# Fused attention and FFN on one core: the first Wo product and the second half of the values leave the bank they share with the score maxima

## Chip, cores and metric

One NeuronCore of a Trainium2 chip. The time is device microseconds of one launch, the median of several runs; lower is better. TensorE (PE) multiplies, PEld is its weight load, VectorE is DVE, ScalarE is ACT, GpSimd is POOL, SyncE is SP.

## The reference

A block of a transformer in float32 over x of 4 x 1024 x 128: attention with 16 heads of 64, added to x, then a gated FFN of width 352 whose inputs and weights are quantised to FP4 and back in blocks of 16, added again.

```python
q, k, v = heads(ln(x) @ Wq.T), heads(ln(x) @ Wk.T), heads(ln(x) @ Wv.T)
attn = exp(s - max(s)); attn /= sum(attn) + 1e-10      # s = q k^T / 8
x = x + (attn @ v) @ Wo.T + bo
h = silu(fp4(ln(x)) @ fp4(w_gate).T) * (fp4(ln(x)) @ fp4(w_up).T)
x = x + fp4(h) @ fp4(w_down).T
```

Every row's maximum is subtracted before the exponential, so it has to be computed from the scores before the scores are computed again, transposed, for the exponential.

## The kernel before

The unit of work is a pair of heads of one batch: 4 batches x 8 pairs = 32 pairs, one round each (r = 1 to 32), with a round 0 ahead that only prepares and a round 33 behind that only finishes. All values are split in a high and a low half-precision part, so that a product is made of several matmuls.

A round has four units k = 0 to 3 (two heads, two halves of 512 query rows) and every unit eight slots s = 0 to 7 (128 keys each). A place in a round is written (k, s). In every slot:

- TensorE computes the transposed scores (L628, L630) into one of two banks `st`, ScalarE takes their exponential (L781), GpSimd its low part (L475). TensorE also multiplies the unit before by the values (L650, L655, L657) into the bank `ob`.
- In slots 0 and 4, TensorE first computes plain scores of the unit ahead for the maxima (`scores`, L610): two pairs of matmuls, each over two banks of the four of `sm`: the first pair in banks 2 and 3, the second in banks 0 and 1. VectorE reduces each pair to a row maximum (L959, written to `negm`) in slots 0, 1, 4 and 5.

Everything else is a **job** of the list `JOBS`: its name, its bank, and its places on TensorE, on ScalarE and on VectorE. There are three banks for jobs: `MB` is their own; `X0` and `X1` are banks 2 and 3 of `sm`, shared with the plain scores. A job is issued at the end of its slot on TensorE (`job`). ScalarE takes it ahead of its exponential of that slot, VectorE behind its reduction of that slot (the two functions `take`). All engines work through these places in program order.

What a job waits for on TensorE is worked out from the list. `job_before` finds the job that had its bank last, and `maxima_ahead` the last maximum taken from the shared banks. In `MB` a job waits until the job before it has been taken (`taken`). In `X0` and `X1` it waits for whichever came later, the job before or the first maximum of the last pair (L533 to L537). In turn `scores` waits until the last jobs in X0 and X1 have been taken (L599 to L602).

The jobs that the change and the prediction speak of:

- `m`: transposes of the maxima (L577), at slot 0 of each unit, in MB; ScalarE and VectorE take it (L732, L920), and SyncE places it by DMA.
- `t0`, `t1`: transposes of the finished outputs' halves (L559), in X1, taken by ScalarE (`oT`, L716). `t1` is at (1, 5).
- `o0`, `o1`: the Wo product of each half (L564), four products, added to x by VectorE (L940). `o0` needs `t0`'s copy.
- `v0`, `v1`: the halves of the next pair's values (L553), 12 matmuls each, the high part taken by ScalarE (L719), then the low part by VectorE (L925).
- `x` (in even rounds from 10) and `h0` (in odd rounds from 11): transposes for the FFN (L1253, L1264), taken by ScalarE (L1276; L1281 and L1282). The FFN of two tiles of rows is spread over two or three rounds, an even one and the odd ones about it; its quantisation runs on VectorE (`quant`, L1088 on) at fixed places, such as (0, 2), (0, 3), (0, 6), (1, 2), (1, 3) and the next round's for the hidden values (`AT_H`), and (3, 6) for their first steps (`AT_H_BEGIN`).
- `w0`, `w1`, `w2`: transposes of the quantised FFN weights in rounds 5, 7 and 8 (L1172, L1170).

Of the kernel before, what the change touches and what calls it, by code (L numbers as in the profile page):

```python
# [49 lines left out]
MB, X0, X1 = range(3)  # L50
JOBS = [("m", MB, (0, 0), (0, 1), (0, 0)), ("k0", X0, (0, 1), (0, 2), (0, 2)), ("k1", MB, (0, 2), (0, 3), (0, 3)),
        ("q0", MB, (0, 4), (0, 5), (0, 5)), ("q1", X0, (0, 5), (0, 6), (0, 6)),
        ("m", MB, (1, 0), (1, 1), (1, 0)), ("t0", X1, (1, 1), (1, 2), None), ("x", MB, (1, 3), (1, 4), None),
        ("o0", X0, (1, 5), None, (1, 6)), ("t1", X1, (1, 5), (1, 6), None), ("h0", MB, (1, 6), (1, 7), None),
        ("m", MB, (2, 0), (2, 1), (2, 0)), ("g0", X0, (2, 1), (2, 2), (2, 2)), ("h1", X1, (2, 1), (2, 2), None),
        ("w0", X1, (2, 1), (2, 2), None), ("w2", X1, (2, 1), (2, 2), None), ("u0", X1, (2, 2), None, (2, 3)),
        ("o1", MB, (2, 3), None, (2, 4)), ("d", X0, (2, 5), None, (2, 6)), ("n0", X0, (2, 5), (2, 6), (2, 6)),
        ("m", MB, (3, 0), (3, 1), (3, 0)), ("g1", X0, (3, 1), (3, 2), (3, 2)), ("w1", X1, (3, 1), (3, 2), None),
        ("n1", X1, (3, 1), (3, 2), (3, 2)), ("u1", X1, (3, 2), None, (3, 3)), ("v0", MB, (3, 3), (3, 4), (3, 4)),
        ("v1", X0, (3, 5), (3, 6), (3, 6))]  # L60
ON_PE, ON_ACT, ON_DVE = 2, 3, 4


# [1438 lines left out]
```

How the kernel before makes its waits and increments, by code:

```python
def wait(eng, sem, n):  # L87
    if isinstance(n, int) and n <= 0:
        return
    eng.wait_ge(sem, n)
# [259 lines left out]
            def round_(g, r, q):  # L351
# [3 lines left out]
                    head, half = (k + 1) // 2 % 2, (k + 1) % 2
                    n, u = 2 * (q if k < 3 else 1 - q) + head, (k + 1) % 2
                    wait(sp, s_mr, 4 * (g - 1) + k + 2)
                    for part, rows in enumerate((m_high, m_low)):
                        sp.dma_start(q_hm[n][part:part + 1, half * HALF:(half + 1) * HALF]
                                     .rearrange("a (t i) -> a t i", t=IT), rows[u][:, :]).then_inc(s_md[u], 16)
                if r == 0:
                    sp.wait_ge(s_qz, 4)
                if cur:
                    place_max(0)
                if nxt:
# [35 lines left out]
        @block.gpsimd  # L404
        def _(pool):
            pool.memset(half[:, :], -0.5).then_inc(s_hf, 1)
            pool.memset(minus[:, :], -1.0).then_inc(s_hf, 1)
            pool.memset(eps[:, :], LN_EPS).then_inc(s_hf, 1)
            pool.memset(ident[:, :], 0.0).then_inc(s_id, 1)
            pool.wait_ge(s_id, 1)
            pool.affine_select(out=ident[:, :], in_=ident[:, :], compare_op=ALU.not_equal, fill=1.0,
                               base=0, pattern=[[-1, P]], channel_multiplier=1).then_inc(s_id, 1)
            for n in range(4):
# [2 lines left out]
                pool.memset(q_hm[n][0:DH, :].bitcast(F32), 0.0).then_inc(s_qz, 1)  # L416
            ffn.constants(pool)
            pool.wait_ge(s_hf, 3)
```

## Time and profile before

| | |
|---|---|
| median of 3 runs | 1441.13 us (1439.35 to 1445.4) |
| the profiled execution | 1440.82 us |
| its span, first to last instruction | 1437.8 us |
| mean granted TensorE clock | 0.982 of full speed |
| busy: PE, DVE, ACT, POOL | 1341.8 (93%), 1123.0 (78%), 1134.4 (79%), 1143.5 us (80%) |
| chain that ended last, by engine | PE 69%, DVE 21%, ACT 6%, issue 3% |

PE is the busiest engine, but a busy share is an average. Which engine holds up the others is seen from the waits and the timeline: for every instruction they give the idle time of its engine ahead of it, and whose work ended it.

### The profile page before, as it was taken

To read this page: it belongs to the slowest core of one execution; us is meant where nothing else is said; L and a number is where in the kernel's file an instruction comes from. 1 tells how busy PE (TensorE), PEld (TensorE's weight loads), DVE (VectorE), ACT (ScalarE), POOL (GpSimd) and SP (SyncE) were. 2 spreads that over 40 slices of the span, in tenths; PEclk is the share of its full clock that TensorE was granted. 3 is DMA by queue.
4 is the path that set the end of the run, shared out by engine and by line. 5 is a ranking of instruction groups with operands and counts; after the bars stand their busy time and mean duration, and the time that the engine had idled before them with its cause. 6 is when DMAs were issued, how large, how long until landed. Compare 5 with 4: busy or idle time off the path is not lost.

```text
span 1437.8 us, 43018 instructions
## 1 busy us (share of the span) xinstructions
PE 1341.8 (93%) x17924; PEld 880.5 (61%) x17924; DVE 1123.0 (78%) x1717; ACT 1134.4 (79%) x2285; POOL 1143.5 (80%) x1135
## 2 busy tenths in 40 slices
PE   3899999999999999999999999999999999999956
PEld 2466666666666666666666666666666666666644
DVE  7777777778778878787887878888787888878677
ACT  2698887978888887888788888888888888788842
POOL 5688988878888878788887888888888888888832
PEclk8899999999999999999999999999999999999986
DMA  7111111112211111122111111211122121112000
GB/s 178 46 46 46 46 41 28 28 42 46 46 46 46 29 44 28 46 50 46 46 28 34 40 46 45 50 35 38 24 49 46 46 50 24 42 31 50 2 5 15
DMA packets 46687, 60.26 MB, mean 42 GB/s; under 512 B 8672, under 2 KB 21920, under 8 KB 46496
## 3 DMA queue, kind: packets, MB, share of 16 engines
q1 hardware_dynamic: 46336, 57.26, 17.0%
q8 instruction: 143, 2.34, 0.7%
q14 instruction: 48, 0.39, 0.1%
q10 hardware_dynamic: 160, 0.26, 0.1%
HBM read 4.80 MB, written 2.10 MB: 5 GB/s over the span
## 4 chain that ended last, share of the span: by engine, by line
PE 69%; DVE 21%; ACT 6%; issue 3%; DMA 1%; POOL 1%; SPq 0%; DVEq 0%
PE st L628 13%; PE st L630 11%; DVE negm L959 8%; PE sm L610 8%; PE ob L650 7%; PE ob L657 6%; PE ob L655 6%; ACT probs L781 3%; PE sm L548 2%; PE sm L1258 2%; PE mb L564 2%; PE sm L564 2%; DVE qv L1113 2%; PE mb L548 2%; PE sm L553 2%
## 5 line engine op out<-in xcount | busy, mean ns | idle before, releaser
L475 POOL TENSOR_TENSOR p_low<-probs 128x512 f16<-128x512 f32 x1024 | 1080.3, 1075 | 231.7 <-ACT probs L781 214.2
L781 ACT ACTIVATE probs<-st,lift,exp_scale 128x512 f32<-128x512 f32 x1024 | 775.3, 772 | 164.2 <-PE st L630 156.3
L959 DVE TENSOR_REDUCE negm<-sm 128x1 f32<-128x1024 f32 x512 | 616.2, 1214 | 204.8 <-PE sm L610 204.5
L628 PE MATMUL st<-q_hl,k_hh 128*128 128x512 f16 x1024 | 391.9, 383 | 6.8 <-ACT probs L781 6.7
L630 PE MATMUL st<-q_hm,k_l 128*128 128x512 f16 x1024 | 388.9, 380 | 0.0
L655 PEld LDWEIGHTS ob<-v,probs 128*128 128x128 bf16 x4096 | 289.7, 99 | 60.9 <-ACT o_raw L750 1.1
L655 PE MATMUL ob<-v,probs 128*128 128x65 f16 x4096 | 319.3, 193 | 0.7 <-ACT o_raw L750 0.7
L657 PE MATMUL ob<-v,probs 128*128 128x64 f16 x4096 | 319.8, 194 | 0.0
L657 PEld LDWEIGHTS ob<-v,probs 128*128 128x128 bf16 x4096 | 270.6, 97 | 59.9
L650 PEld LDWEIGHTS ob<-v,p_low 128*128 128x128 f16 x4096 | 177.1, 97 | 90.7 <-issue 1.1
L628 PEld LDWEIGHTS st<-q_hl,k_hh 128*128 128x128 f16 x1024 | 99.5, 97 | 154.3 <-issue 80.4
L650 PE MATMUL ob<-v,p_low 128*128 128x65 f16 x4096 | 188.1, 193 | 0.0
L610 PE MATMUL sm<-k_hh,q_hl 64*128 64x512 f16 x512 | 155.7, 384 | 10.7 <-DMA q_hm<-q_high 3.8
L610 PE MATMUL sm<-k_hh,q_hm 64*128 64x512 f16 x512 | 156.2, 385 | 0.0
L791 ACT ACTIVATE o_n<-o_raw,rden 128x64 f32<-128x64 f32 x512 | 147.1, 337 | 1.1 <-DVE rden L948 1.1
L630 PEld LDWEIGHTS st<-q_hm,k_l 128*128 128x128 f16 x1024 | 100.2, 98 | 26.8 <-issue 9.5
L716 ACT ACTIVATE oT<-sm 128x512 f32<-128x512 f32 x64 | 38.2, 597 | 37.4 <-PE sm L559 37.0
L946 DVE TENSOR_SCALAR den<-o_raw 128x4 f32<-128x4 f32 x128 | 51.4, 402 | 8.4 <-ACT o_raw L750 8.4
L564 PE MATMUL sm<-wo_s,oT 128*128 128x128 f32 x256 | 36.8, 287 | 20.7 <-DVE negm L959 19.3
L610 PEld LDWEIGHTS sm<-k_hh,q_hl 64*128 64x128 f16 x512 | 29.1, 94 | 34.5 <-issue 11.2
L750 ACT ACTIVATE o_raw<-ob 128x260 f32<-128x260 f32 x128 | 50.0, 390 | 0.0
L564 PEld LDWEIGHTS sm<-wo_s,oT 128*128 128x128 f32 x256 | 31.2, 192 | 22.5 <-DVE negm L959 20.9
(204 smaller groups left out, 1640.6 us busy)
## 6 DMA issues: line engine op xcount, KB each, us to landing
k_hh<-k_high SPq DMA_DIRECT2D x128, 128.0 KB, 2.4
k_l<-k_low SPq DMA_DIRECT2D x64, 128.0 KB, 2.4
q_hl<-q_high SPq DMA_DIRECT2D x64, 128.0 KB, 2.3
q_hl<-q_low SPq DMA_DIRECT2D x64, 128.0 KB, 2.4
q_hm<-q_high SPq DMA_DIRECT2D x62, 128.0 KB, 2.3
x<-x SPq DMA_DIRECT2D x4, 512.0 KB, 7.3
q_hm<-m_high SPq DMA_DIRECT2D x128, 1.0 KB
q_hm<-m_low SPq DMA_DIRECT2D x128, 1.0 KB
```

Source lines behind the costliest of these rows:

```text
L475: return pool.tensor_tensor(p_low[b][:, j, :], p, p.bitcast(BF16)[:, 1::2], ALU.subtract)
L548: last = pe.matmul(bank[:, :], of_pair(wT[w], "qk".index(name[0]), g), of_batch(xT[a], g, c * HALF, HALF), start=(w == 0 and a == 0), stop ...
L564: last = pe.matmul(bank[:, t * P:(t + 1) * P], oT[:, (4 * c + t) * P:(4 * c + t + 1) * P], wo_s[:, bass.ds((g - 2) % PAIRS, 1), :].rearran ...
L610: last = pe.matmul(sm_banks[2 * (1 - a) + h], q_rows[rows, t * P:(t + 1) * P], k_hh[n][rows, h * 512:(h + 1) * 512], start=True, stop=True)
L628: pe.matmul(st[s % 2][:, :], k_hh[n][:, s * P:(s + 1) * P], q_hl[n][:, half * HALF:(half + 1) * HALF], start=True, stop=False)
L630: pe.matmul(st[s % 2][:, :], k_l1[n][:, s * P:(s + 1) * P], q_hm[n][:, half * HALF:(half + 1) * HALF], start=False, stop=True).then_inc(s_ ...
L650: last = pe.matmul(ob[:, o:o + VC], p_low[1 - k % 2][:, j, t * P:(t + 1) * P], v_j[:, 1:1 + VC], start=False, stop=(j == JT - 1), skip_gro ...
L655: pe.matmul(ob[:, o:o + VC], p, v_j[:, 1:1 + VC], start=(t == 0 and j == 0), stop=False, skip_group_check=True)
L657: pe.matmul(ob[:, o + 1:o + VC], p, v_j[:, 1 + VC:1 + VC + DH], start=False, stop=False, skip_group_check=True)
L781: nc.scalar.activation(probs[k % 2][:, s, :], st[s % 2][:, :], ACT.Exp, bias=lift[:, 0:1], scale=exp_scale[:, head, pair:pair + 1]).then_i ...
L791: last = nc.scalar.activation(o_n[pq][:, tile + t, head * DH:(head + 1) * DH], o_raw[k % 2][:, t, 1:VC], ACT.Copy, scale=rden[:, k % 2, t: ...
L959: nc.vector.tensor_reduce(negm[k % 2][:, pair % 4:pair % 4 + 1], banks.rearrange("p a n -> p (a n)"), AX.X, ALU.max, negate=True).then_inc ...
```

## The change

Four jobs change bank or place, and no instruction is added or removed. The first Wo product `o0` goes from X0 in slot 5 to MB in slot 4 of unit 1, and its addition on VectorE from slot 6 to slot 5. The second half of the values `v1` goes from X0 in slot 5 to MB in slot 6 of unit 3, and is taken in slot 7 in place of 6. To make room in MB, the transposes `x` come one slot earlier, and `h0` goes from MB to X0 at its old place.

```diff
-        ("m", MB, (1, 0), (1, 1), (1, 0)), ("t0", X1, (1, 1), (1, 2), None), ("x", MB, (1, 3), (1, 4), None),
-        ("o0", X0, (1, 5), None, (1, 6)), ("t1", X1, (1, 5), (1, 6), None), ("h0", MB, (1, 6), (1, 7), None),
+        ("m", MB, (1, 0), (1, 1), (1, 0)), ("t0", X1, (1, 1), (1, 2), None), ("x", MB, (1, 2), (1, 3), None),
+        ("o0", MB, (1, 4), None, (1, 5)), ("t1", X1, (1, 5), (1, 6), None), ("h0", X0, (1, 6), (1, 7), None),
...
-        ("v1", X0, (3, 5), (3, 6), (3, 6))]
+        ("v1", MB, (3, 6), (3, 7), (3, 7))]
```

## Rows read from the trace of the kernel before

**Rows 1.** Waits of TensorE: us in total, times, longest us.

```profile
PE sm L564 <- DVE negm L959: 19.3, 13, 2.4
PE sm L553 <- DVE negm L959: 9.0, 13, 1.1
```

**Rows 2.** Timeline, round 23, (1, 5) to (2, 0): start, us, engine, line, operation.

```profile
968.61 0.38 PE L628 MATMUL st<-q_hl,k_hh 128*128 128x512 f16 x1
...
969.88 2.34 DVE L959 TENSOR_REDUCE negm<-sm 128x1 f32<-128x1024 f32 x2
...
971.15 1.16 PE L564 MATMUL sm<-wo_s,oT 128*128 128x128 f32 x8 [1.45 <-DVE negm L959]
...
972.58 0.38 PE L628 MATMUL st<-q_hl,k_hh 128*128 128x512 f16 x1
...
974.20 0.27 ACT L1282 ACTIVATE hiddenT<-mb 96x128 f32<-96x128 f32 x1
...
974.62 0.09 PEld L610 LDWEIGHTS sm<-k_hh,q_hl 64*128 64x128 f16 x1
...
975.06 1.23 DVE L959 TENSOR_REDUCE negm<-sm 128x1 f32<-128x1024 f32 x1 [2.03 <-PE sm L610]
```

**Rows 3.** Timeline, round 32, (2, 3): the second Wo product, with nothing beside it.

```profile
1356.52 1.13 PE L564 MATMUL mb<-wo_s,oT 128*128 128x128 f32 x8
...
1357.49 0.38 PE L628 MATMUL st<-q_hl,k_hh 128*128 128x512 f16 x1
```

**Rows 4.** Timeline, round 23, the products of (3, 5), (3, 6) and (3, 7).

```profile
991.04 0.38 PE L628 MATMUL st<-q_hl,k_hh 128*128 128x512 f16 x1
...
992.64 0.67 DVE L925 TENSOR_TENSOR v<-mb,v 128x512 f16<-128x512 f32 x1
...
992.78 0.23 PE L553 MATMUL sm<-wT_high,xT_high 128*128 128x128 f16 x1 [0.66 <-DVE negm L959]
...
993.46 0.38 PE L628 MATMUL st<-q_hl,k_hh 128*128 128x512 f16 x1
...
994.13 0.38 PE L628 MATMUL st<-q_hl,k_hh 128*128 128x512 f16 x1
```

**Rows 5.** Timeline, round 24, (3, 5) to the next round's (0, 0).

```profile
1033.27 0.38 PE L628 MATMUL st<-q_hl,k_hh 128*128 128x512 f16 x1
...
1033.61 0.68 DVE L925 TENSOR_TENSOR v<-mb,v 128x512 f16<-128x512 f32 x1
...
1034.21 1.22 DVE L959 TENSOR_REDUCE negm<-sm 128x1 f32<-128x1024 f32 x1
...
1034.85 0.38 PE L628 MATMUL st<-q_hl,k_hh 128*128 128x512 f16 x1
...
1035.68 0.69 DVE L925 TENSOR_TENSOR v<-sm,v 128x512 f16<-128x512 f32 x1 [0.26 <-ACT v L719]
...
1036.29 0.88 DVE L1103 TENSOR_REDUCE q_small<-hidden 128x44 f32<-128x704 f32 x1
...
1037.20 0.28 DVE L1105 TENSOR_SCALAR q_small<-q_small 128x44 f32<-128x44 f32 x1
...
1037.40 0.09 PEld L577 LDWEIGHTS mb<-ident,negm 128*4 128x4 f32 x1
```

**Rows 6.** Timeline, (2, 0) and (2, 1): round 5 (two rows) and round 8.

```profile
222.06 1.23 DVE L959 TENSOR_REDUCE negm<-sm 128x1 f32<-128x1024 f32 x1
...
223.64 0.50 PE L1172 MATMUL sm<-ident,wgu 128*128 128x128 f32 x3
...
345.92 0.55 PE L1170 MATMUL sm<-ident,wd 128*128 128x128 f32 x3 [0.62 <-DVE negm L959]
```

**Rows 7.** Timeline, round 0, (3, 4), to the scores of round 1.

```profile
40.34 0.68 DVE L925 TENSOR_TENSOR v<-mb,v 128x512 f16<-128x512 f32 x1
...
40.48 0.29 PE L553 MATMUL sm<-wT_high,xT_high 128*128 128x128 f16 x1 [1.11 <-DVE negm L959]
...
43.56 0.58 PE L610 MATMUL sm<-k_hh,q_hl 64*128 64x512 f16 x1 [1.61 <-DVE v L925]
```

## The prediction

> **What bounds the kernel now.** I read the waits of TensorE first, then the timeline of one odd and one even round, slot by slot. TensorE is the engine whose idle time counts: it works almost without a gap through all rounds of attention, in program order, so a wait in its queue moves everything behind it. The list of its waits names the two that the change touches [rows 1]: the first Wo product (o0, L564 into the shared bank) stood 19.3 us in 13 rounds, the second half of the values (v1, L553) 9.0 us in 13 rounds, both for a maximum (negm, L959) on VectorE. The other rounds don't wait there at all. Those 28.3 us are about the most that the change could bring; what matters is what each of these instructions would wait for next.
>
> The timeline says where the 13 lie. Eleven of the waits of o0 are in the odd rounds 11 to 31, 1.45 us each [rows 2], where the quantisation of the hidden values has delayed VectorE; the remaining 3.3 us are in rounds 5 and 8. Twelve of the waits of v1 are in the odd rounds 9 to 31, 0.66 us each [rows 4], and one of 1.11 us is in round 0 [rows 7]. I use round 23 for the odd rounds and round 24 for the even ones.
>
> **First Wo product, odd rounds 11 to 31.** The products of slot 5 of unit 1 began at 968.61. VectorE served the two reductions of slot 4 and 5 from 969.88 to 972.22, the first until about 971.09, and o0 started at 971.15 [rows 2]. In its own bank o0 waits for no maximum: it goes in at 968.61, ahead of slot 5, and costs 0.97 us there, which is what the second Wo product takes alone (1356.52 to 1357.49) [rows 3]. Then come the products of slot 5, 0.90 us (a slot 5 with v1 and without a wait takes 1033.27 to 1034.85, 1.58 [rows 5], less 0.68 for v1 [rows 4]). They end at 968.61 + 0.97 + 0.90 = 970.48. **t1 (L559) stays in slot 5 and in the shared bank, so it inherits the wait for the same maximum** and stands until 971.15. It takes 0.46 us (o0 and t1 together took 971.15 to 972.58, 1.43 us [rows 2], less 0.97 for o0), so slot 6 begins at 971.61 in place of 972.58. The gain is 0.97 us a round: the length of o0, not the length of the wait. 11 x 0.97 = 10.7 us.
>
> Is it given back? Behind the two reductions VectorE sat idle for 2.03 us before the next one [rows 2], so a TensorE that comes 0.97 us sooner doesn't run into it. h0 moves the other way, into a shared bank: the scores at the start of unit 2 must now wait until ScalarE has copied it. That copy ended at 974.47 and the scores' weights went in at 974.62 [rows 2]. Both follow t1, so the distance of 0.15 us stays, less some 0.06 us from signal to start (971.09 to 971.15). I take nothing for it; if the cover is gone, the overrun costs in 12 rounds.
>
> In the rounds with no wait the change only takes o0 and t1 apart, on a TensorE that works on either side of them: same matmuls, nothing. The transposes x come one slot sooner in even rounds: same instructions, on a bank that ScalarE and VectorE have left two slots before, nothing. The addition of o0 on VectorE goes from slot 6 to slot 5, behind the same two reductions: nothing. No DMA moves, and SyncE's and GpSimd's lists stay as they are.
>
> **Rounds 5 and 8.** In both, VectorE has a quantisation of weights queued behind these reductions without a break, and TensorE meets it again in unit 2. In round 8 the transposes of w_down then stand 0.62 us for the next maximum [rows 6]: what o0 gives is paid there, gain 0. In round 5 that next maximum comes from 222.06 to 223.29 [rows 6] after a queue without idle time; the transposes behind it went in at 223.64 [rows 6], so TensorE can save some 0.35 us and no more. Between 0 and 0.97 us in each; I take 0.4 for the two.
>
> **Second half of the values, odd rounds 9 to 31.** It went in behind slot 5 and now goes in behind slot 6, into the own bank. Slot 5 with v1 takes 1.58 us without the wait [rows 5], and 2.42 in odd rounds (991.04 to 993.46) [rows 4]: the wait costs 0.84. After the change v1 is ready to go at 991.04 + 0.90 + 0.67 (slot 6, 993.46 to 994.13) = 992.61, and no maximum is in its way. But **the own bank still holds v0**, the first half: VectorE takes its low part from 992.64 to 993.31 [rows 4]. v1 starts at 993.37, takes 0.68, and slot 7 begins at 994.05 in place of 994.13. Of 0.84 us 0.08 are left: 12 x 0.08 = 1.0 us. In even rounds v0 has been taken by 1034.29, before v1 is ready at 1034.85 [rows 5]: no wait, no gain.
>
> The Trainium skill, page "PSUM — Partial Sum Buffer", section "Summary: rules for kernel authors", says that reading PSUM while matmuls run wants the matmuls in a different bank, and semaphores by bank. That speaks against this half of the change, since v0 and v1 had two banks and now share one. By that rule v1 comes out as above, 1.0 us; without it, with only the maximum in the way, it would be the first rival.
>
> What is late next: the transposes of the maxima (m, L577) at slot 0 of the next round use v1's new bank. In even rounds VectorE now has two steps of 0.88 and 0.28 us ahead of v1's low part; its reduction ends at 1035.43, so the low part (0.68) ends at 1037.15 to 1037.27, and m's weights went in at 1037.40 [rows 5]. That is a cover of 0.1 to 0.2 us: nothing, but thin. In odd rounds v1 is through at 994.05; copy and low part took 1.52 us behind it (1034.85 to 1036.37) [rows 5], so the bank is free at 995.6, while m comes 1.88 us after the start of slot 7 (1034.85 + 0.67 to 1037.40) [rows 5], at 995.9.
>
> **Round 0.** v1 waited for a maximum until 40.48 and the scores of round 1 for v1's low part, 1.61 us, until 43.56 [rows 7]. So v1 itself took 43.56 - 1.61 - 40.48 = 1.47 us. Now v1 waits for v0's low part (until 41.02 [rows 7]), is through at 41.08 + 1.47 = 42.55, and the scores follow at once: 1.0 us, between 0 and 1.6.
>
> **Sum.** 10.7 + 0.4 + 1.0 + 1.0 = 13.1 us. The profiled execution took 1440.8 us (its span 1437.8, and 3.0 around it), 0.3 under the median of 1441.1. 1441.1 - 13.1 = **1428.0 us**. About 0.5% (7.2 us) is what a measurement of this kernel can tell from no change, so "faster" means under 1433.9.
>
> **Rivals.** First, both waits go altogether for v1: 0.84 us in 12 rounds, 9.1 us more than I count: 1418.9. Against it: v0's low part stands in VectorE's list behind the late maximum [rows 4]. Chance 0.07.
> Second, the handover at the round's end costs: m waits for v1's low part. With 0.2 us beyond the cover in 31 rounds, 6.2 us: 1434.2, no change by the bound above. For it: the thin cover in rows 5. Chance 0.11.
> Third, h0's copy holds the scores of unit 2 by 0.1 to 0.4 us in 12 rounds, 1.2 to 4.8 us: 1429.2 to 1432.8. For it: the 0.15 us of rows 2. Chance 0.07.
> Fourth, on the other side: v1's low part comes late by about the length of a reduction (1.22 us [rows 5]). ScalarE copies the high part only after an exponential, VectorE waits for that copy, and its next reduction waits behind. m, the reduction and all that follows on TensorE would stand about 1.0 us in 31 rounds: 1428 + 31 = 1459. It decides from (13.1 + 7.2) / 31 = 0.65 us a round on. Against it: before the change both came within 1.52 us of v1's end, and 1.88 us are there now [rows 5]. Chance 0.04.
>
> **How the numbers follow.** Forecast 0.71. The range takes in the forecast, the third rival, the second up to its price and part of the way to the first, since the prices of round 0 and of rounds 5 and 8 could add up to 2.1 us: 1421 to 1434.5. Faster by over 0.5%: the forecast, the first and the third, 0.85. Within 0.5%: the second, 0.11. Slower: the fourth, 0.04.
>
> **What would show it.** In rounds 11 to 31 o0 starts right behind slot 4 with no idle time, and t1 in slot 5 has an idle time of about 0.6 us for negm. v1, now into mb, has an idle time of about 0.6 us in odd rounds, put down to v0's low part (L925), and none for a maximum. m has no idle time. Odd rounds from 11 on get 1.0 us shorter and even rounds keep their length. Idle time at m, or at the scores of unit 2 for L1282, would make me wrong.

## The result, and the profile after

The changed kernel took **1457.78 us** (median of 4 runs, 1454.72 to 1459.94), the kernel before beside it 1440.24 us (4 runs, 1439.06 to 1445.4). The ratio is 1.0121 with a 95% interval of 1.0106 to 1.0136: slower by 17.5 us, where 13.1 us less was forecast. The profiled execution took 1454.72 us, the shortest of the four; its span is 1452.9 us (1437.8 before), the mean granted clock of TensorE 0.982 as before. The other three show a mean granted clock of 0.979 to 0.980.

The page of the changed kernel, busy time by engine and the chain that ended last:

```profile
PE 1347.8 (93%) x17924; PEld 881.0 (61%) x17924; DVE 1160.9 (80%) x1717; ACT 1141.2 (79%) x2285; POOL 1140.0 (78%) x1135
PE 59%; DVE 31%; ACT 5%; issue 3%; DMA 1%; POOL 1%; SPq 0%; DVEq 0%
```

No instruction was added, and yet VectorE is busy 1160.9 us in place of 1123.0. Its share of the chain that ended last went from 21% to 31%, TensorE's from 69% to 59%. The 37.9 us of additional busy time are the trail to follow: **the same steps last longer.** First the waits of TensorE, in the changed kernel (us in total, times, longest us):

```profile
PE mb L548 <- DVE k_low L914: 21.9, 12, 2.8
PE mb L553 <- DVE v L925: 8.7, 13, 1.7
PE sm L559 <- DVE negm L959: 6.6, 12, 1.4
PE sm L1172 <- DVE negm L959: 3.8, 2, 2.8
PE mb L577 <- DVE v L925: 2.9, 11, 0.3
```

and of the kernel before, the two lines beside [rows 1] that answer to them:

```profile
PE mb L548 <- DVE k_low L914: 4.7, 12, 2.8
PE sm L1172 <- DVE negm L959: 0.9, 1, 0.9
```

The two waits of [rows 1], 28.3 us, are gone. t1 (L559) and v1 (L553) wait 6.6 and 8.7 us in their place. The new one is large and stands at a job that the change did not touch: **q0**, the first projection of the queries at slot 4 of unit 0 (L548 into the jobs' own bank), waits 21.9 us for the low part of k1 (L914), 4.7 before. The transposes of the maxima (m, L577) wait 2.9 us.

Where the rounds gained and lost, from the slots' starts (first L628 of each) in the two traces (means over the odd rounds 11 to 29 and the even rounds 10 to 30; round 31 of the changed kernel is an exception, 45.61 us):

| stretch | before | after |
|---|---|---|
| odd rounds from 11: slots (1, 4) and (1, 5) | 4.66 | 3.72 us |
| odd rounds: slots (3, 5) and (3, 6) | 3.09 | 3.01 |
| odd rounds: slot (1, 7), ahead of the scores that follow h0 | 1.55 | 1.62 |
| end of an odd round: (3, 7) and the next (0, 0) | 2.26 | 2.33 |
| end of an even round: (3, 7) and the next (0, 0) | 2.20 | 2.53 |
| odd rounds: slot (0, 4), with q0 | 1.68 | 3.24 |
| a whole odd round | 43.29 | 44.24 |
| a whole even round from 10 | 41.34 | 41.61 |
| round 0, from the span's start | 44.53 | 43.27 |
| round 5 | 42.94 | 45.21 |
| round 8 | 40.67 | 41.30 |

**Rounds 5 and 31 hold something else as well, the granted clock.** From the first slots of round 1 to the end of round 31 TensorE's granted clock is 1.00, but for a few short stretches at 0.50, the lower of its two levels (1.2 in place of 2.4 GHz). The kernel before has one, in round 5, in slots 5 to 7 of unit 1 (first line; the number ahead of the last two is the granted clock). The changed kernel has two, in round 5 at (2, 3) and in round 31 at (0, 4) and (0, 5):

```profile
217.70:221.00 3.30, 3.30 (x19) 2.15 (x19) 3.16 (x9) 1.96 (x3) 1.22 (x2) 0.50 0.00 0
224.30:227.60 3.30, 3.30 (x27) 2.80 (x24) 0.27 (x1) 1.58 (x4) 2.61 (x4) 0.50 0.00 1
1313.20:1316.50 3.30, 3.30 (x23) 1.72 (x22) 3.27 (x4) 2.16 (x3) 0.31 (x2) 0.50 0.56 130
```

With it slot (2, 3) of round 5 took 4.14 us in place of 2.53, and round 31 1.4 us more than the other odd rounds. Shortly ahead of the first TensorE had stood 2.83 us for a maximum, just ahead of the second 1.73 us for k1's low part; but the same waits stand in other rounds and runs with no such stretch behind them. So rounds 5 and 8 can't be compared by their lengths alone. The run with the cut in unit 3 alone, below, has the same instructions as the changed kernel up to round 8. There round 5 has no such stretch and takes 43.60 us, and round 8 has one and takes 42.87.

**The part of o0 went as forecast.** Round 23 of the changed kernel, TensorE from slot 4 to slot 6 of unit 1 (start us, us, then the instruction; in brackets the idle time ahead of it and what ended it):

```profile
978.68 0.39 PE L628 MATMUL st<-q_hl,k_hh 128*128 128x512 f16 x1
979.38 1.13 PE L564 MATMUL mb<-wo_s,oT 128*128 128x128 f32 x8
980.35 0.38 PE L628 MATMUL st<-q_hl,k_hh 128*128 128x512 f16 x1
981.91 0.66 PE L559 MATMUL sm<-ident,o_n 128*128 128x128 f32 x4 [0.48 <-DVE negm L959]
982.40 0.38 PE L628 MATMUL st<-q_hl,k_hh 128*128 128x512 f16 x1
```

o0 has no idle time ahead of it, t1 waits the rest of what o0 used to wait. Against [rows 2], with 0.69 us for slot 4, the two slots are 0.94 us shorter (0.97 forecast).

**The part of v1** takes the wait that was forecast, but VectorE behind it looks different. Round 23 again, slot 5 of unit 3 to the next round:

```profile
1002.52 0.68 DVE L925 TENSOR_TENSOR v<-mb,v 128x512 f16<-128x512 f32 x1
1003.17 2.04 POOL L475 TENSOR_TENSOR p_low<-probs 128x512 f16<-128x512 f32 x2 [0.40 <-ACT probs L781]
1003.25 0.23 PE L553 MATMUL mb<-wT_high,xT_high 128*128 128x128 f16 x1 [0.58 <-DVE v L925]
1004.25 1.25 DVE L1128 SCALAR_TENSOR_TENSOR qv<-qw,qv 128x256 f32<-128x256 f32 x1
1005.41 0.68 DVE L925 TENSOR_TENSOR v<-mb,v 128x512 f16<-128x512 f32 x1
1006.15 0.27 PE L577 MATMUL mb<-ident,negm 128*4 128x128 f32 x1
```

v1 waits 0.58 us for v0's low part. But the step of the quantisation between the two low parts, L1128, lasts 1.25 us; behind v1's low part, as it stood before the change, it lasted 0.41. It now ends 0.29 us after the second of two instructions of GpSimd that began at 1003.17. Here it still fits: m goes in at 1006.15 without idle time.

**In even rounds it doesn't fit.** The end of round 24 and what follows in round 25:

```profile
1045.36 0.88 DVE L1103 TENSOR_REDUCE q_small<-hidden 128x44 f32<-128x704 f32 x1
1046.23 1.04 POOL L475 TENSOR_TENSOR p_low<-probs 128x512 f16<-128x512 f32 x1
1046.27 1.05 DVE L1105 TENSOR_SCALAR q_small<-q_small 128x44 f32<-128x44 f32 x1
1047.23 0.68 DVE L925 TENSOR_TENSOR v<-mb,v 128x512 f16<-128x512 f32 x1
...
1047.96 0.27 PE L577 MATMUL mb<-ident,negm 128*4 128x128 f32 x1 [0.26 <-DVE v L925]
...
1051.76 0.71 DVE L1109 TENSOR_SCALAR q_small<-q_small 128x44 f32<-128x44 f32 x1
1052.95 1.04 POOL L475 TENSOR_TENSOR p_low<-probs 128x512 f16<-128x512 f32 x1 [0.52 <-ACT probs L781]
1052.97 1.77 DVE L1113 TENSOR_TENSOR qv<-hidden,q_small 128x704 f32<-128x704 f32 x1
1054.66 0.74 DVE L914 SCALAR_TENSOR_TENSOR k_low<-mb,k_scale,k_high 128x512 f16<-128x512 f32 x1
1055.46 0.39 PE L548 MATMUL mb<-xT_high,wT_high 128*128 128x512 f16 x1 [1.73 <-DVE k_low L914]
```

The same place before, VectorE and GpSimd (L1105 itself, 1037.20 and 0.28, is in [rows 5]):

```profile
1036.40 1.04 POOL L475 TENSOR_TENSOR p_low<-probs 128x512 f16<-128x512 f32 x1
...
1040.92 0.17 DVE L1109 TENSOR_SCALAR q_small<-q_small 128x44 f32<-128x44 f32 x1
1041.59 1.17 DVE L1113 TENSOR_TENSOR qv<-hidden,q_small 128x704 f32<-128x704 f32 x1
```

Set the starts against GpSimd's. L1105 began 0.04 us after an instruction of GpSimd (1046.23) and ended at 1047.32, 0.05 us after its end. Before, it began at 1037.20, 0.80 us into the instruction of 1036.40, and ended at 1037.48, 0.04 us after its end. **Both times it ended with GpSimd's instruction; 0.28 us was what was left of that, not what the step costs.** The groups by shape say that it is so in every round (us in total, mean ns), in the kernel before:

```profile
L1105 DVE TENSOR_SCALAR q_small<-q_small 128x44 f32<-128x44 f32 x12 | 4.0, 330 | 0.4
L1109 DVE TENSOR_SCALAR q_small<-q_small 128x44 f32<-128x44 f32 x12 | 2.8, 236 | 0.0
L1113 DVE TENSOR_TENSOR qv<-hidden,q_small 128x704 f32<-128x704 f32 x12 | 13.7, 1139 | 0.4
L1128 DVE SCALAR_TENSOR_TENSOR qv<-qw,qv 128x256 f32<-128x256 f32 x12 | 4.9, 409 | 0.0
```

and in the changed one:

```profile
L1105 DVE TENSOR_SCALAR q_small<-q_small 128x44 f32<-128x44 f32 x12 | 12.4, 1034 | 0.4
L1109 DVE TENSOR_SCALAR q_small<-q_small 128x44 f32<-128x44 f32 x12 | 8.7, 726 | 0.0
L1113 DVE TENSOR_TENSOR qv<-hidden,q_small 128x704 f32<-128x704 f32 x12 | 20.4, 1703 | 0.4
L1128 DVE SCALAR_TENSOR_TENSOR qv<-qw,qv 128x256 f32<-128x256 f32 x12 | 14.9, 1244 | 0.0
```

Nor is there an exception in the traces of all thirteen kernels. Every L1105 and L1109 of 128 x 44 elements that took over 0.23 us, 169 in all, ended 0.04 us after the instruction of GpSimd that was running when it began. The larger steps end later by a fixed part of their own work: L1128 (128 x 256) by 0.28 us, L1131 and L1135 (128 x 384) by 0.41 or 0.42, L1113 (128 x 704) by 0.74 or 0.75.

The four groups above are 31.0 us of the additional busy time. L1105, L1109 and L1113 stand ahead of the low part of k1 on VectorE, and q0 needs that low part.

### The profile page after: what moved, and what is told of

Same layout as the page of the kernel before. It is cut to its first block, busy times and chain, and to the rows that moved or that the text cites. A ratio compares the mean times of both kernels' runs of the same rounds, so it can differ in the third digit from the quotient of the medians.

```text
span 1452.9 us, 42989 instructions
## 1 busy us (share of the span) xinstructions
PE 1347.8 (93%) x17924; PEld 881.0 (61%) x17924; DVE 1160.9 (80%) x1717; ACT 1141.2 (79%) x2285; POOL 1140.0 (78%) x1135
## 4 chain that ended last, share of the span: by engine, by line
PE 59%; DVE 31%; ACT 5%; issue 3%; DMA 1%; POOL 1%; SPq 0%; DVEq 0%
DVE negm L959 12%; PE st L628 11%; PE st L630 9%; PE sm L610 6%; PE ob L657 5%; PE ob L655 5%; PE ob L650 5%; ACT probs L781 3%; PE mb L564 3%; DVE qv L1113 2%; PE sm L1258 2%; PE sm L548 2%; DVE v L925 2%; PE mb L548 2%; DVE qv L1128 2%
## 5 line engine op out<-in xcount | busy, mean ns | idle before, releaser
L959 DVE TENSOR_REDUCE negm<-sm 128x1 f32<-128x1024 f32 x512 | 615.6, 1213 | 199.1 <-PE sm L610 199.0
L628 PE MATMUL st<-q_hl,k_hh 128*128 128x512 f16 x1024 | 392.0, 383 | 7.1 <-ACT probs L781 6.9
L628 PEld LDWEIGHTS st<-q_hl,k_hh 128*128 128x128 f16 x1024 | 99.6, 97 | 151.8 <-issue 81.1
L564 PE MATMUL mb<-wo_s,oT 128*128 128x128 f32 x512 | 73.4, 287 | 1.4 <-ACT oT L716 1.4
L946 DVE TENSOR_SCALAR den<-o_raw 128x4 f32<-128x4 f32 x128 | 63.2, 493 | 9.0 <-ACT o_raw L750 9.0
L564 PEld LDWEIGHTS mb<-wo_s,oT 128*128 128x128 f32 x512 | 63.1, 194 | 1.7 <-issue 1.7
L553 PE MATMUL mb<-wT_high,xT_high 128*128 128x128 f16 x256 | 46.9, 221 | 10.2 <-DVE v L925 8.7
L925 DVE TENSOR_TENSOR v<-mb,v 128x512 f16<-128x512 f32 x64 | 43.5, 680 | 8.5 <-ACT v L719 8.5
```

What stands on the lines that cost most here:

```text
L564: last = pe.matmul(bank[:, t * P:(t + 1) * P], oT[:, (4 * c + t) * P:(4 * c + t + 1) * P], wo_s[:, bass.ds((g - 2) % PAIRS, 1), :].rearran ...
L628: pe.matmul(st[s % 2][:, :], k_hh[n][:, s * P:(s + 1) * P], q_hl[n][:, half * HALF:(half + 1) * HALF], start=True, stop=False)
L925: nc.vector.tensor_tensor(part[:, :, :, 2 + DH:2 + 2 * DH], bank[:, :].rearrange("p (t h d) -> p t h d", t=4, h=2), part[:, :, :, 2:2 + DH ...
L959: nc.vector.tensor_reduce(negm[k % 2][:, pair % 4:pair % 4 + 1], banks.rearrange("p a n -> p (a n)"), AX.X, ALU.max, negate=True).then_inc ...
```

## The experiments

Two theories for where the loss comes from: A, v1's move; B, o0's and h0's. Then for the mechanism: C, the steps of VectorE about v1's low part are held by GpSimd's running instruction; D, its rivals as the expectations name them. The last three runs ask which of the held steps matter. All times are medians with their range, all ratios are against the kernel before in the same comparison, with a 95% interval. Where an edit adds lines, the traces' line numbers behind it are larger by 2.

**o0, x and h0 alone.** v1 as before:

```diff
-           ("v1", MB, (3, 6), (3, 7), (3, 7))]
+           ("v1", X0, (3, 5), (3, 6), (3, 6))]
```

> The o0 part alone: o0, x and h0 where the change puts them, v1 as before in the shared bank at slot 5. Theory A (all the loss comes from v1's new place): the odd rounds 11 to 31 gain 0.95 us each as in the trace of after, h0's copy costs 0.07 us in them, rounds 5 and 8 lose 2.3 and 0.6 us as there; 1440.8 - 10.4 + 0.8 + 2.9 = about 1434 us, and the wait of q0 (L548) for k1's low part in odd rounds is back at 0.2 us. Theory B (the loss comes from o0 or h0 in their new banks): 1450 us or more, with that wait at 1.7 us.

1435.03 us (1434.54 to 1435.59), ratio 0.9966 (0.9953 to 0.9979). The wait of q0 in its list of waits is what it was before:

```profile
PE mb L548 <- DVE k_low L914: 4.4, 12, 2.6
```

Odd rounds are 0.89 us shorter than before, even ones the same within 0.07. This half of the change is a gain. Rounds 5, 7 and 8 lose 2.33, 0.48 and 0.71 us of it; in rounds 5 and 7 this trace has a stretch at a granted clock of 0.50, which in round 5 makes slots (2, 2) and (2, 3) 1.6 us longer.

**v1 alone.** The other half:

```diff
-        ("v1", X0, (3, 5), (3, 6), (3, 6))]
+        ("v1", MB, (3, 6), (3, 7), (3, 7))]
```

> The v1 part alone, o0, x and h0 as before. Theory A: it carries more than the whole loss, 13.9 + 6.7 = 20.6 us over before, about 1461 us, with the wait of L548 for k1's low part at about 1.7 us in odd rounds and m (L577) waiting 0.26 us for v1's low part. Theory B: about 1440 us.

1463.56 us (1461.99 to 1468.83), ratio 1.0174 (1.0147 to 1.0202).

```profile
PE mb L548 <- DVE k_low L914: 21.3, 12, 2.3
```

q0's wait comes with v1's move and with nothing else. The two halves nearly add up, -0.3% and +1.7% against +1.2% together. A holds, B falls. Only round 5 is 2.3 us longer with either half, and some 1.5 us of that is again the clock (slot (2, 3) takes 4.03 us in place of 2.53, at 0.50).

**Shorter instructions on GpSimd, in the changed kernel.** If GpSimd's instruction holds VectorE, it must hold it for less when it is short:

```diff
+SHORT = ((3, 4), (3, 5), (3, 6), (3, 7), (0, 0), (0, 1), (0, 2), (0, 3), (0, 4))
...
-                            low_part(k % 2, s).then_inc(s_lp, 1)
+                            short = r >= 9 and (k, s) in SHORT
+                            low_part(k % 2, s, 8 if short else HALF).then_inc(s_lp, 1)
```

> The changed kernel, with GpSimd's low parts of the exponentials cut to 8 of 512 columns from round 9 on in slots 4 to 7 of unit 3 and slots 0 to 4 of unit 0 (the low parts of the other columns there are left over from earlier rounds, so the output is not the reference's). Theory C (VectorE's small steps L1105, L1109, L1128 and L1113 are held until GpSimd's instruction of 1.04 us ends): L1105 falls from 1.05 to under 0.3 us, L1128 from 1.25 to 0.41, m waits for nothing, and the wait of q0 in odd rounds falls from 1.7 us to under 0.2; against the kernel before with the same cut it is then about 10 us faster. Theory D (VectorE is late only by the order of its list): the durations stay, and it is 15 us slower than the kernel before with the same cut.

1425.68 us (1424.93 to 1427.97), ratio 0.9902 (0.9884 to 0.9919): 32 us less than the changed kernel, with TensorE's and VectorE's lists untouched. L1105 now takes 0.19 us, L1109 0.18, L1113 0.89 and L1128 0.41. The wait of m is gone, q0 waits in one round only.

**The same cut in the kernel before:**

> The kernel before with the same cut of GpSimd's low parts: the yardstick for the run above. Theory C: 4 to 8 us under the kernel before, since the waits of 0.34 us at slot 4 and 0.19 us at slot 5 of unit 0 in odd rounds go, and with them perhaps the wait for a maximum in unit 3. Theory D: as before, within 1 us.

1438.93 us (1436.87 to 1440.14), ratio 0.9991 (0.9982 to 1.0001). I had expected it 4 to 8 us faster; it gained about one. That was a miss: in the kernel before the held steps were not on the path. It makes the comparison cleaner. GpSimd's work in these slots costs the kernel before next to nothing, and 32 us only in the order of the changed one. With the cut, the changed kernel is 13.3 us faster than the one before: **a gain of the size forecast is there once GpSimd no longer holds VectorE in these slots**.

**The quantisation's steps behind v1's low part.** In the changed kernel, the steps of (3, 6) moved to slot 7:

```diff
-AT_X, AT_X_END = ((2, 7), (3, 2), (3, 3), (3, 6)), ((0, 2), (0, 6))
-AT_H_BEGIN, AT_H = ((3, 6),), ((0, 2), (0, 3), (0, 6), (1, 2), (1, 3))
+AT_X, AT_X_END = ((2, 7), (3, 2), (3, 3), (3, 7)), ((0, 2), (0, 6))
+AT_H_BEGIN, AT_H = ((3, 7),), ((0, 2), (0, 3), (0, 6), (1, 2), (1, 3))
```

> The changed kernel with the quantisation steps of slot 6 of unit 3 (L1103 and L1105 in even rounds, L1128 in odd ones) moved to slot 7, which puts them behind v1's low part in VectorE's list. Theory C (the step ahead of v1's low part is held by GpSimd, and that alone makes VectorE late): m waits for nothing and q0's wait in odd rounds is back under 0.3 us; 1428 to 1435 us. Theory D (VectorE owes the same work at the round's end in any order, so its lateness stays): m's wait goes but q0 still waits over 1 us in odd rounds; about 1450 us.

1439.21 us (1437.42 to 1440.19), ratio 0.9986 (0.9977 to 0.9995). The waits of m and q0 are gone (q0 4.8 us, as before), which C asks for, but the time is 4 us above its range, since k0 now waits:

```profile
PE sm L548 <- DVE negm L959: 8.3, 11, 0.8
```

The steps now stand ahead of the reduction that frees the shared bank for k0. v1's low part had to be ahead of the steps, and the reduction too; one of the two is always behind in this order.

**L1105 alone moved**, in the changed kernel, for the hidden values only, from (3, 6) to (0, 2):

```diff
+        late = part != ALL_BUT_LAST and width == 2 * FF
+        if part == ALL_BUT_LAST or part == int(late):
             dve.wait_ge(q, at + 1)
             nc.vector.tensor_scalar(scale, amax, 1.0 / 6.0, 1e-12, ALU.mult, ALU.max).then_inc(q, 1)
```

> The changed kernel with one instruction of 44 columns, L1105 for the hidden values, moved from slot 6 of unit 3 to slot 2 of unit 0 of the next round. Theory C: ahead of v1's low part there is only the reduction L1103, which GpSimd never held in the traces (0.88 us each time); m's wait of 0.26 us in odd rounds goes, q0 waits between 0.2 and 1.2 us instead of 1.7, and the time is 1437 to 1449 us; the 0.28 us of even rounds stay, since L1128 is still ahead. Theory D: an instruction of 44 columns makes no difference, 1455 to 1458 us.

1448.9 us (1447.92 to 1449.66), ratio 1.0056 (1.0041 to 1.0071), 9 us less than the changed kernel. m no longer waits, and even rounds keep their 0.28 us, as expected, but q0 still waits:

```profile
PE mb L548 <- DVE k_low L914: 21.3, 12, 2.3
```

The time is at the edge of C's range, but the count for q0, 0.2 to 1.2 us a round, was missed: it waits 1.73 us, as in the changed kernel. The step has left v1's low part alone and still stands ahead of k1's. It takes 0.18 us there, and behind it L1109 takes 0.92 us and L1113 1.77 (0.71 and 1.77 in the changed kernel). So the end of the even round is on time here, and one short step more ahead of L1109 is enough to bring the holds in unit 0 back. My notion that m's wait was the main part was too simple.

**h0 left in the own bank**, on the kernel with o0 alone:

```diff
-        ("o0", MB, (1, 4), None, (1, 5)), ("t1", X1, (1, 5), (1, 6), None), ("h0", X0, (1, 6), (1, 7), None),
+        ("o0", MB, (1, 4), None, (1, 5)), ("t1", X1, (1, 5), (1, 6), None), ("h0", MB, (1, 6), (1, 7), None),
```

> The o0 part alone, with h0 left in the own bank. Is the third piece of the change needed? h0 must then wait there until VectorE has added o0 to x, which in odd rounds follows its two reductions (done near slot 5's end) by 0.7 us: a wait of about 0.7 us in 12 rounds less 0.07 us that h0's copy no longer costs, 1435 + 7.5 = about 1442 us. If VectorE's addition is early enough, 1434 us.

1442.26 us (1440.26 to 1445.33), ratio 1.0012 (1.0002 to 1.0022). As expected, h0 then waits for the addition of o0, which stands behind two reductions:

```profile
PE mb L1264 <- DVE x L940: 4.8, 12, 0.5
```

So h0's move is a needed part of o0's gain: 0.54 us in each odd round, 5.9 of the 7.2 us between the two medians, at a price of 0.06 us in each odd round. Round 8 is 1.6 us longer here too, but no h0 runs in it; this trace has a granted clock of 0.50 at its slot (2, 3) and the other has not.

**Both halves of the values early**, on the kernel with o0 alone, so that both low parts are through before the steps of slot 6:

```diff
-        ("n1", X1, (3, 1), (3, 2), (3, 2)), ("u1", X1, (3, 2), None, (3, 3)), ("v0", MB, (3, 3), (3, 4), (3, 4)),
-        ("v1", X0, (3, 5), (3, 6), (3, 6))]
+        ("n1", X1, (3, 1), (3, 2), (3, 2)), ("u1", X1, (3, 2), None, (3, 3)), ("v0", MB, (3, 2), (3, 3), (3, 3)),
+        ("v1", MB, (3, 4), (3, 5), (3, 5))]
```

(In round 0 the steps that prepare v0 come a slot earlier with it.)

> The o0 part, and both halves of the values in the own bank but earlier: v0 in slot 2 (taken in slot 3), v1 in slot 4 (taken in slot 5) of unit 3. v1 then waits neither for the late maximum nor for v0's low part, and its own low part stays ahead of the quantisation steps of slot 6. If the wait removed is a gain whenever VectorE's list keeps its order behind it: 0.84 us in 12 rounds less than the o0 part alone, about 1425 us. If VectorE's total work at the round's end decides: 1435 us.

1428.28 us (1426.98 to 1428.8), ratio 0.9912 (0.9897 to 0.9927), 3 us above the first of the two times. **This beats both kernels and computes all of the reference.** v1 has the own bank and no wait for a maximum, odd rounds are 1.43 us shorter than before, even ones 0.1 longer. Round 8 loses 2.4 us, 1.6 of them in slot (2, 3), where the granted clock is 0.50; most of the rest it loses with o0 alone as well.

**Which link makes q0 wait?** The held step at the end of the even round, or those in unit 0 of the odd one? Twice the changed kernel with the cut of above in a part of the slots. Unit 0 only:

```diff
-SHORT = ((3, 4), (3, 5), (3, 6), (3, 7), (0, 0), (0, 1), (0, 2), (0, 3), (0, 4))
+SHORT = ((0, 2), (0, 3), (0, 4))
```

> The changed kernel, but from round 9 on GpSimd makes only 8 of 512 columns of its low parts in slots 2, 3 and 4 of unit 0 (the rest is left out). In round 25 of the changed kernel L1109 took 0.71 us (0.17 before) and L1113 1.77 (1.17 before, 0.89 with GpSimd idle) ahead of k1's low part. If it is these two holds that make q0 wait (1.73 us in the odd rounds), the low part comes up to 1.4 us sooner: q0's wait falls to 0.2 to 0.6 us, total 5 us or less in its list of waits, and the time to 1438 to 1445 us. If the delay is handed down from the end of the round before (v1's low part and the step held there), the wait stays at 1.2 us or more and the time at 1452 or more. The wait of m (2.9 us in 11 rounds) stays either way.

1438.57 us (1436.98 to 1439.23), ratio 0.9991 (0.9982 to 1.0), in the range of the holds in unit 0.

```profile
PE mb L550 <- DVE k_low L916: 6.5, 12, 3.1
```

and unit 3 only:

```diff
-SHORT = ((3, 4), (3, 5), (3, 6), (3, 7), (0, 0), (0, 1), (0, 2), (0, 3), (0, 4))
+SHORT = ((3, 4), (3, 5), (3, 6), (3, 7))
```

> The changed kernel, but from round 9 on GpSimd makes only 8 of 512 columns of its low parts in slots 4 to 7 of unit 3 (the rest is left out). L1105 in slot 6 of even rounds took 1.05 us; it should take 0.2 to 0.3, v1's low part come 0.8 us sooner, and m's wait of 2.9 us in 11 rounds go. If the delay at q0 is handed down from there, its wait (21.9 us) falls under 8 us and the time to 1436 to 1442 us. If the holds in unit 0 make it, it stays at 15 to 22 us and the time at 1446 to 1453 us (even rounds 0.3 and odd rounds 0.3 us shorter).

1426.76 us (1426.29 to 1428.03), ratio 0.9912 (0.9897 to 0.9926), within 1.1 us of the cut in all nine slots, and 9 us under the range that I gave a delay handed down: I had counted q0's wait and m's idle time, and odd rounds fell by 2.1 us, even ones by 0.33.

```profile
PE mb L550 <- DVE k_low L916: 4.7, 12, 2.8
```

The groups of VectorE by shape in this kernel (L1107, L1111 and L1115 are L1105, L1109 and L1113):

```profile
L1107 DVE TENSOR_SCALAR q_small<-q_small 128x44 f32<-128x44 f32 x12 | 3.0, 246 | 0.4
L1111 DVE TENSOR_SCALAR q_small<-q_small 128x44 f32<-128x44 f32 x12 | 2.1, 175 | 0.0
L1115 DVE TENSOR_TENSOR qv<-hidden,q_small 128x704 f32<-128x704 f32 x12 | 13.6, 1136 | 0.4
```

In unit 0 GpSimd works in full here, and L1111 and L1115 still take 0.18 and 1.14 us, as in the kernel before. So the long holds in unit 0 are not a second cause: **they follow from the late end of the round before**, which puts these steps just behind GpSimd's starts. Either cut breaks the chain, since q0's wait needs both links here: the one in unit 0 gives 19 us back, the one in unit 3 all 31. That a late end is not the only way into the holds of unit 0, the run with L1105 moved has shown.

**Round 5.** The cut in rounds 5 and 8 alone, in slots 4 to 7 of unit 1 and 0 and 1 of unit 2:

```diff
+SHORT = ((1, 4), (1, 5), (1, 6), (1, 7), (2, 0), (2, 1))
...
+                            short = r in (5, 8) and (k, s) in SHORT
```

> The changed kernel, but in rounds 5 and 8 GpSimd makes only 8 of 512 columns of its low parts in slots 4 to 7 of unit 1 and 0 and 1 of unit 2 (what is left out is the rest of these low parts, so its instructions there are short). Round 5 took 42.94 us before and 45.21 after; its L1131 and L1135 took 0.56 us each before and 1.28 after, while GpSimd's instructions lie back to back. If GpSimd's running instruction holds VectorE there too (theory C), both steps take 0.56 us or less, the transposes of the weights wait 1.4 us or less in place of 2.83, and round 5 takes 42.5 to 43.9 us. If it is the new order of VectorE's list in slots 5 and 6 (the addition ahead of the steps), round 5 stays at 45.0 or above. All other rounds unchanged; 1455 us by C, 1458 by the other.

Round 5 of the changed kernel, VectorE, GpSimd and the transposes of the weights:

```profile
216.84 6.19 POOL L475 TENSOR_TENSOR p_low<-probs 128x512 f16<-128x512 f32 x5 [3.11 <-ACT probs L781]
218.55 1.28 DVE L1131 SCALAR_TENSOR_TENSOR qv<-qw,qv 128x384 f32<-128x384 f32 x1
222.86 0.52 PE L1172 MATMUL sm<-ident,wgu 128*128 128x128 f32 x3 [2.83 <-DVE negm L959]
```

and with the cut:

```profile
220.19 0.56 DVE L1133 SCALAR_TENSOR_TENSOR qv<-qw,qv 128x384 f32<-128x384 f32 x1
223.06 0.52 PE L1174 MATMUL sm<-ident,wgu 128*128 128x128 f32 x3 [1.39 <-DVE negm L961]
```

Round 5 falls to 41.32 us, under the 42.94 of before and under my lower bound of 42.5; round 8 to 39.32 (40.67 before). The time is 1452.14 us (1451.68 to 1454.12), ratio 1.0085 (1.0068 to 1.0102), 5.6 us less than the changed kernel, 3 less than I expected. The steps were held in round 5 too, as theory C has it. But this trace has no stretch at a granted clock of 0.50 in rounds 5 and 8, so the 3.9 us between 45.21 and 41.32 are not all the hold's. Against the 43.60 us of round 5 without such a stretch the cut gives 2.3 us. And of the 2.3 us by which the change made round 5 longer, about 0.7 came with the holds (43.60 against 42.94, a round with a stretch of its own in another place) and 1.6 with the clock at (2, 3). The kernel before paid for holds as well: its L1113 took 1.44 us in this round, 0.59 with the cut.

## Why the prediction was wrong

**The step that failed** is the cover of m at the round's end: "In even rounds VectorE now has two steps of 0.88 and 0.28 us ahead of v1's low part [...] That is a cover of 0.1 to 0.2 us: nothing, but thin." The 0.88 held. The 0.28, read from the row of L1105 in [rows 5], was taken for the step's own length, and became 1.05. v1's low part ended 2.37 us after the start of slot 7 (1045.54 to 1047.91), where the working had 1.63 to 1.75, and the 0.1 to 0.2 us of cover were gone. What stood behind it were m's 4.3 us and, through the longer holds in unit 0, q0's 17.2 us.

- **o0**: right in the odd rounds. 0.94 us a round against 0.97; t1 inherited the wait, 0.48 us where about 0.6 was said. Alone it took 1435.03 us, 4.3 less than before; rounds 5, 7 and 8 took 3.5 us back, part of it by the clock.
- **h0's cover**: the scores of unit 2 start 0.06 us later in odd rounds. The 0.15 us did not quite cover it; the third rival's price of at least 0.1 us was not reached.
- **Rounds 5 and 8**: sign wrong. +0.4 us of gain was forecast within 0 to 0.97 each; they lost 2.3 and 0.6. "TensorE can save some 0.35 us and no more" took VectorE's queue as fixed in length; two of its steps in round 5 went from 0.56 to 1.28 us when TensorE came sooner, and the transposes of the weights began 0.74 us later in the round. The other 1.6 us of round 5 are the granted clock at (2, 3), which the prediction has no term for.
- **v1**: right in itself. It waits 0.58 us for v0's low part, and the two slots are 0.08 us shorter, as forecast.
- **Round 0**: right. From v0's start to the first slot of round 1 it took 5.44 us (37.84 to 43.27) in place of 6.52 (38.00 to 44.53), 1.08 shorter, 1.0 forecast. The rest of the 1.26 us in the table is an earlier start of v0; that start lies between 37.8 and 39.7 us in the runs here, whatever the change.
- **m**: wrong in both kinds of rounds, +0.06 us behind an odd and +0.33 behind an even round, 4.3 us in all. The second rival named this place and 6.2 us for it; its price was about right, and it would still not have made the kernel slower.
- **q0**: not in the prediction at all. 1.56 us in each of the odd rounds from 11, 17.2 us, more than the whole forecast gain. The working followed the lateness of v1's low part to the next job in its bank and stopped there. It did not follow VectorE's list on into unit 0.
- The **fourth rival** gave about the right time, 1459, by luck: its mechanism is another. It had v1's low part late by a reduction behind ScalarE's copy and some 1.0 us lost at m in every round. The traces show 0.26 us at m and the large wait four slots further on, in odd rounds alone.

Rounds 13, 21 and 29 of the run with the cut in rounds 5 and 8 are 1.4 us longer than their like, as round 31 of the changed kernel is, and in each the granted clock is 0.50 in slots (0, 4) and (0, 5), right behind q0's wait. The kernel before has no such stretch between rounds 6 and 31. Whether the other three executions of the changed kernel, 2.3 to 5.2 us longer than the profiled one, had more of them is not shown, since their traces aren't kept; their lower mean clock speaks for it. Open is what decides in which round the clock falls.

## What to carry to other kernels

The duration of a VectorE step in a profile may include the time in which it was held by GpSimd's running instruction: before a sum uses it, look at the same step where GpSimd is idle and at its start against GpSimd's. A step that ends with GpSimd's instruction, or whose length differs between rounds, costs anything between its own length and that plus GpSimd's, and every shift of TensorE or VectorE deals it anew. So don't move a job whose bank is wanted soon behind such a step, and where a step gets later, follow its engine's list to the next handover that has no slack, not only to the next user of the bank.

## What the runs showed of the hardware

I had not expected one engine's instruction to set the end of another's with no data between them. L1105 (128 x 44 elements) takes 0.18 us in the kernel's last stretch, where GpSimd is idle beside it, 0.28 when 0.80 us of GpSimd's 1.04 are over, and 1.04 to 1.05 when it begins with it. L1109 (128 x 44) went from 0.17 to 0.71, L1113 (128 x 704) from 1.17 to 1.77, L1128 (128 x 256) from 0.41 to 1.25. It works the other way too: in round 5 five instructions of GpSimd took 6.19 us, and the three beside L1128, L1131 and L1135 took 1.35 to 1.41 each, where one takes 1.04. The reductions were never held (L1103 0.87 to 0.89 and L959 1.18 to 1.23 in all thirteen traces, whatever GpSimd did), nor was L925 (0.67 to 0.69), which reads one of its inputs from PSUM.

The Trainium skill has the rule, on the page "SBUF — State Buffer", section "Who interferes with whom". VectorE and GpSimd share one pair of ports as an exclusive lock, and the first to issue has it for its whole instruction while the other "fully blocks". A VectorE instruction with two inputs in SBUF contends with a GpSimd instruction that reads SBUF. One with at most one such input, outside the two-port modes, does not. `tensor_scalar` can contend when it runs in such a mode, and a `tensor_reduce` never does on this chip. This case's traces agree: held were L1113, L1128, L1131 and L1135 (two inputs in SBUF) and L1105 and L1109 (`tensor_scalar`), not held L1103, L959 and L925. Which mode a `tensor_scalar` ran in they don't show. The page was not weighed against the row of L1105 in the prediction. Its rule would have made a rival of its own there: a full instruction of GpSimd, 1.04 us, in place of 0.28, and m's cover at 0.2 - 0.8 = -0.6 us, an estimate; m then waited 0.26 us.

The granted clock fell to 0.50 and rose again within one round, with the same instructions up to that round: round 5 took 45.21 us with such a stretch at (2, 3) and 43.60 without, round 8 42.87 with it and 41.30 without. Such a stretch made a round 1.4 to 1.6 us longer. So the granted clock in the window of a round is to be looked at before a step of the program is blamed for a difference of that size.
